# Twelve products with unread results ahead of tile 0's attention, and the prologue in another order

## The reference, cut to what matters

```python
# x: (16, 128, 64, 2); S4D-like token mixing gives h: (16, 128, 1024)
num = exp(dt_Lambda_neg) - 1
den = exp(dt_Lambda_neg * L) - 1
Wc = Wc * num * _reciprocal(den * Lam, EPS)                    # Wc from x
K = einsum('chn,hnl->chl', Wc, exp(dt_Lambda[..., None] * pos - P_max[..., None]))
h = K.real
# masked linear layer on the layer norm, 1024 x 1024, mask in blocks of 32 x 32
w_masked = weight * elem_mask
h = h + einsum('bsk,nk->bsn', _layernorm(h), w_masked)
# base layer 1024 x 1024 + router (8 experts, sparsemax) + LoRA of rank 16
z = _layernorm(h)
h = h + einsum('bsd,od->bso', z, W_base) + b_base + einsum('bser,bse,ero->bso', hA, weights, lora_B)
```

## Time and profile before

| what | us |
| --- | --- |
| median of 3 runs | 519.96 (519.64 to 520.29) |
| the profiled execution, device time | 520.99 |
| its span, first to last instruction | 519.2 |
| PE busy in the span | 480.4 |
| DVE busy | 408.4 |
| ACT busy | 261.4 |
| POOL busy | 125.7 |

### The profile page before, as it was taken

The page is one execution under the profiler, slowest core; times in us unless marked ns, Lnnn a source line. Parts: engine busy times, 40 slices in busy tenths (PEclk is TensorE's granted clock), DMA queues, the critical chain, the costliest instruction groups (busy, mean ns, idle before and its releaser), DMA issues.

```text
span 519.2 us, 7441 instructions
## 1 busy us (share of the span) xinstructions
PE 480.4 (93%) x2467; PEld 406.1 (78%) x2467; DVE 408.4 (79%) x862; ACT 261.4 (50%) x476; POOL 125.7 (24%) x110
## 2 busy tenths in 40 slices
PE   1378789999999999999999999999999999999995
PEld 0267667877888888888888888888888888888884
DVE  7998979898988888888888888888888888854241
ACT  2848887576464626364554646362636455232200
POOL 0765597440303021020303030302102030303020
PEclk9998989999999999999999999999999999999999
DMA  8993113040403031212212030403121211313011
GB/s 286 391 338 51 63 42 122 1 127 6 126 3 110 16 88 38 81 45 68 59 40 86 10 116 0 109 17 88 38 81 47 67 56 26 96 31 92 1 40 40
DMA packets 28764, 40.83 MB, mean 79 GB/s; under 512 B 10760, under 2 KB 21192, under 8 KB 28744
## 3 DMA queue, kind: packets, MB, share of 16 engines
q1 hardware_dynamic: 28368, 40.49, 25.8%
q10 hardware_dynamic: 376, 0.10, 0.1%
HBM read 23.80 MB, written 16.78 MB: 78 GB/s over the span
## 4 chain that ended last, share of the span: by engine, by line
PE 90%; DVE 4%; issue 2%; ACT 2%; DMA 1%; POOL 1%; SPq 0%; DVEq 0%; POOLq 0%; ACTq 0%
PE acc_b L455 38%; PE acc_a L455 34%; PE turnp L439 6%; PE small L479 4%; PE turnp L448 3%; PE small L481 2%; PE acc_b L420 1%; PE acc_b L399 1%; DMA mask_raw<-in_L_attn_mask 1%; PE xps L429 1%; ACT wa_hi L668 1%; DVE mask_sum L1071 0%; DVE wa_raw L1080 0%; DVE wa_lo L1087 0%; PE small L487 0%
## 5 line engine op out<-in xcount | busy, mean ns | idle before, releaser
L982 POOL TENSOR_TENSOR h<-h,st 128x1024 f32<-128x1024 f32 x16 | 30.4, 1897 | 325.1 <-PE turnp L448 321.5
L455 PE MATMUL acc_a<-wa_hi,x_hi 128*128 128x512 f32 x256 | 83.2, 401 | 1.9 <-DVE wa_lo L1087 1.9
L455 PE MATMUL acc_b<-wb_hi,x_hi 128*128 128x512 f32 x256 | 83.9, 404 | 0.0
L455 PE MATMUL acc_a<-wa_hi,x_lo 128*128 128x512 f32 x256 | 81.3, 394 | 0.0
L455 PE MATMUL acc_a<-wa_lo,x_hi 128*128 128x512 f32 x256 | 81.2, 393 | 0.0
L455 PE MATMUL acc_b<-wb_lo,x_hi 128*128 128x512 f32 x256 | 80.5, 390 | 0.0
L455 PE MATMUL acc_b<-wb_hi,x_lo 128*128 128x512 f32 x256 | 80.5, 390 | 0.0
L455 PEld LDWEIGHTS acc_a<-wa_hi,x_lo 128*128 128x128 f32 x256 | 48.6, 190 | 10.4
L752 ACT ACTIVATE x_hi<-turnp 128x1024 fp32r<-128x1024 f32 x16 | 16.4, 1024 | 79.4 <-PE turnp L448 79.4
L455 PEld LDWEIGHTS acc_a<-wa_lo,x_hi 128*128 128x128 f32 x256 | 48.5, 189 | 10.0
L455 PEld LDWEIGHTS acc_b<-wb_hi,x_lo 128*128 128x128 f32 x256 | 48.1, 188 | 10.4
(11 more groups left out here) (200 smaller groups left out, 937.0 us busy)
## 6 DMA issues: line engine op xcount, KB each, us to landing
h<-rows_out SPq DMA_DIRECT2D x16, 512.0 KB, 3.3
out<-h SPq DMA_DIRECT2D x15, 512.0 KB
rows_out<-b_sb SPq DMA_DIRECT2D x56, 128.0 KB, 2.3
mask_raw<-in_L_attn_mask SPq DMA_DIRECT2D x8, 512.0 KB, 9.9
wa_raw<-in_L_attn_weight SPq DMA_DIRECT2D x8, 512.0 KB, 10.5
wb_raw<-in_L_ffn_W_base SPq DMA_DIRECT2D x8, 512.0 KB, 6.7
rows_out<-tmp SPq DMA_DIRECT2D x8, 128.0 KB, 2.3
xn<-in_x SPq DMA_DIRECT2D x15, 64.0 KB
```

Of the source, the lines that this page charges most:

```text
L455: return pe.matmul(cols, a, rows, start=first, stop=last)
L982: pool.tensor_tensor(h2[par][:, :], h2[par][:, :], st2[:, par, 1:2].to_broadcast([P, L]), ALU.subtract)\
```

## The change

A new helper on PE issues fp32 products of the identity with 256 columns of the constants, whose results nobody reads (the first product of tile 0's attention overwrites them):

```diff
+            def keep_clock(bank, n):
+
+                for _ in range(n):
+                    pe.matmul(bank, ident, kst[:, 0:2 * P], start=True, stop=True)
```

Its calls, and the new place of the calls around them on PE:

```diff
             k_transposed(0)
+            block_sums(5)
+            block_sums(6)
             wa_half(6)
             wa_half(7)
-            block_sums(6)
-            block_sums(7)
+            pe.wait_ge(wa_masked, 3)
+            keep_clock(acc_a[:, HALF // 2:HALF], 2)
+            keep_clock(acc_a[:, HALF // 2:HALF], 2)
+            keep_clock(acc_a[:, HALF // 2:HALF], 2)
             wa_half(8)
+            keep_clock(acc_a[:, HALF // 2:HALF], 2)
+            keep_clock(acc_a[:, HALF // 2:HALF], 2)
             wa_half(9)
+            keep_clock(acc_a[:, HALF // 2:HALF], 2)
             pe.wait_ge(kt_lo, 1)
             wa_rows_ready(NWT // 2)
             first_attention(0, [0])
             first_attention(0, [1])
+            block_sums(7)
+            first_attention(0, [2])
             wa_half(10)
-            first_attention(0, [2])
+            x_transposes(1)
             first_attention(0, [3])
```

```diff
             parameters(0)
+            table_b(0)
             phases_1()
-            table_b(0)
```

On DVE nearly every call moves. At the start:

```diff
             dt_exponential()
             signs()
+            dec_and_turn()
+            q_arguments(0)
+            reciprocal_of_tanh(0)
+            phases(0)
             mask_sums(0)
-            dec_and_turn()
-            phases(0)
-            q_arguments(0)
+            mask_sums(1)
             wa_mask(0)
-            reciprocal_of_tanh(0)
```

More of the change, by code:

```diff
@@ L528, in _ @@
             block_sums(0)
+            pe.wait_ge(rt_in, 16)
+            pe.transpose(small[:, HALF - rt_rows:HALF], rt_stage, ident[0:rt_rows, 0:rt_rows]).then_inc(rt_t, 1)
             block_sums(1)
@@ L531, in _ @@
             wa_half(0)
+            wa_half(1)
             block_sums(3)
-            wa_half(1)
+            x_transposes(0)
             block_sums(4)
[L535 to L538, removed]
             wa_half(2)
@@ L588, in _ @@
             attention(1, 0)
+            wb_half(6)
+            wb_half(7)
+            attention(1, 1)
             wb_half(8)
             wb_half(9)
-            attention(1, 1)
             attention(1, 2)
@@ L602, in _ @@
             attention(1, 6)
+            wb_half(13)
+            wb_half(14)
             attention(1, 7)
-            wb_half(14)
             wb_half(15)
+            k_transposed(2)
             pe.wait_ge(h2t_lo, 1)
@@ L612, in _ @@
             base(0, 0)
+            x_transposes(3)
             base(0, 1)
@@ L779, in _ @@
             q_tanh(0)
+            x_rows_twice(0)
+            q_sines(0)
+            sines(0)
+            exponentials(0)
+            wa_centre(0)
+            wa_highs(0)
             act.wait_ge(ldt_in, 16)
@@ L797, in _ @@
             wa_highs(4)
+            x_rows_twice(1)
+            exponentials(1)
             wa_highs(5)
+            wa_centre(4)
             k_high(0)
@@ L802, in _ @@
             wa_raws(3)
+            wa_centre(5)
             wa_highs(8)
-            x_rows_twice(1)
             wa_highs(9)
-            exponentials(1)
-            wa_centre(5)
+            q_tanh(1)
             sines(1)
@@ L813, in _ @@
             wa_highs(13)
-            q_tanh(1)
             wa_highs(14)
             wa_highs(15)
[L817 to L822, removed]
             k_sum(0)
             k_deviation(0)
+            wb_highs(0)
             q_sines(1)
+            x_rows_twice(2)
+            k_high(1)
+            wb_highs(1)
             wb_highs(2)
             wb_highs(3)
-            k_high(1)
+            sines(2)
             wb_highs(4)
@@ L851, in _ @@
             act.activation(lb_hi[:, :], lb_raw[:, :], ACT.Copy).then_inc(lorb_hi, 1)
-            k_high(2)
+            sines(3)
+            gated_high(0)
             exponentials(3)
-            gated_high(0)
-            sines(3)
             h2_deviation(1, 1)
@@ L1298, in _ @@
             signs()
+            dec_and_turn()
+            q_arguments(0)
+            reciprocal_of_tanh(0)
+            phases(0)
             mask_sums(0)
-            dec_and_turn()
-            phases(0)
-            q_arguments(0)
+            mask_sums(1)
             wa_mask(0)
-            reciprocal_of_tanh(0)
-            mask_sums(1)
             mask_sums(2)
             mask_sums(3)
+            decay_b(0)
+            reciprocal_of_norm(0)
             wa_mask(1)
-            reciprocal_of_norm(0)
-            mask_sums(4)
+            wa_lows(0)
+            v_factors(0)
             wa_mask(2)
             wa_mask(3)
-            wa_mask(4)
-            decay_b(0)
-            v_factors(0)
+            mask_sums(4)
+            wa_lows(1)
             mask_sums(5)
-            wa_lows(0)
-            wa_lows(1)
             table_v(0)
             mask_sums(6)
+            wa_mask(4)
             wa_lows(4)
             wa_lows(5)
+            phases(1)
+            q_arguments(1)
+            k_low(0)
             mask_sums(7)
             wa_mask(5)
-            phases(1)
-            k_low(0)
             wa_mask(6)
+            k_turn(0)
             wa_lows(8)
+            wa_mask(7)
             wa_lows(9)
-            q_arguments(1)
-            wa_mask(7)
             decay_b(1)
-            k_turn(0)
+            reciprocal_of_tanh(1)
             wa_lows(12)
@@ L1341, in _ @@
             wb_lows(0)
+            phases(2)
+            k_low(1)
             wb_lows(1)
-            phases(2)
-            reciprocal_of_tanh(1)
+            wb_lows(2)
             h1_reciprocal(0)
-            wb_lows(2)
             wb_lows(3)
@@ L1349, in _ @@
             attention_residual(0, 0)
-            k_low(1)
             wb_lows(4)
             wb_lows(5)
+            k_turn(1)
             wb_lows(6)
+            router_columns()
             wb_lows(7)
-            k_turn(1)
+            decay_b(2)
+            reciprocal_of_norm(1)
             wb_lows(8)
             wb_lows(9)
-            reciprocal_of_norm(1)
+            v_factors(2)
             wb_lows(10)
+            table_v(2)
             wb_lows(11)
             wb_lows(12)
+            h2_low(0)
             wb_lows(13)
[L1363 to L1366, removed]
+            h2_reciprocal(0, 0)
             wb_lows(14)
             wb_lows(15)
+            h1_reciprocal(1)
             phases(3)
-            h2_reciprocal(0, 0)
-            h1_reciprocal(1)
             dve.wait_ge(b_ready, 3)
```

53 lines of the change are left out of this document (21 added, 32 removed).

## The result

The changed kernel takes 521.86 us (median of 7 runs, 520.23 to 523.54); the kernel before, beside it, 519.96 (7 runs, 519.63 to 520.55). The ratio is 1.0035, with a 95% interval of 1.0018 to 1.0052: a loss of 0.35%, small, but the interval leaves out 1. The forecast was 516.5. The profiled execution took 521.86 us with a span of 520.1 (before: 520.99 and 519.2).

A forecast was written before the change was run, and what follows sets the result against it. TensorE is busy from 118.02 us on, so only idle and half-clock time before it can move: -1.5 + (7.5 - 7.6) + (1.7 - 3.4) = -3.3, and 0.2 for POOL: -3.5 from 519.96 gives 516.5 us, range 514.3 to 520.3.

The forecast's parts named there:

- Part 1: The start, on DVE: v_sb ends at 29.6, k_transposed(0) starts at about 29.7 and ends at 33.1, 3.3 us earlier.
- rival D: At the start, everything waits for xn on ACT's queue: slower, 522.5 us if it lands at 17.1; chance 0.08.
- Part 2: Twelve multiplications ahead of tile 0's attention cost 1.7 of the 3.2 us gained; attention starts at 40.6, -1.5 us.
- rival B: Clock still low in the twelve multiplications, so attention starts near 43.7: 518.5 us; chance 0.17.
- Part 3: Tile 0's attention to k_transposed(1): wb_half(0) at 51.7 after 2.0 us idle; k_transposed(1) waits 2.5 us for b_sb(1), at 56.7.
- Part 4: From k_transposed(1) to 118 us: waits of 2.35, 0.88 and 1.20 us go, new ones of 1.6 us come.
- the step in part 4: At wb_half(13): table_v(2) waits for tile 1's rows, DVE loses 1.1 us, yet wb_lows(11) is done at 80.2.
- the booked fall: One half-clock spell on PE behind the idle times 49.7 to 51.7 and 54.2 to 56.7, costing 1.7 us.
- the small waits: New PE waits after k_transposed(1): 0.3 us for the residual, then 0.4, 0.4, 0.3, 0.2 at wb_half(8) to (11); 1.6 us.
- Rival C: At k_transposed(3), DVE or the rows' round trip is late, 3.5 us idle, prologue's gain lost: 519.9 us; chance 0.10.
- The last paragraph of the prediction: What the profile after would show, and what could be wrong: a DVE queue running later than counted beside other POOL work.

The follow-up runs named there:

- the lower group of times: Changed kernel with POOL's additions in table_b(2) and add_bias waiting for DVE: two executions at 514.89 and 514.96 us, the other four at 516.73 to 516.86.

## Why the prediction was wrong

**Right**, by its parts. Part 1: v_sb(0) ends at 29.22 (forecast 29.6), k_transposed(0) starts at 29.41 (29.7); xn held nobody up, so rival D is out. Part 2: a product of 256 columns takes about 0.46 us at the upper clock (0.445), the rows of all twelve add up to 5.7 us (5.3), and rival B did not occur. Without them attention starts at 38.94, where 38.9 was forecast; with them at 39.62 and not 40.6, so they cost 0.7 us and not 1.7. Part 3: wb_half(0) at 51.33 (51.7), k_transposed(1) at 56.39 behind 2.37 us (56.7, 2.5). Part 4 up to DVE's wait for tile 1's rows: attention(1, 0) waits 0.35 us for the residual (0.3), the rows are there at 76.01 (75.9). No wait ahead of wb_half(6), and no fall at 43 or 70.

**Wrong: the step in part 4** by which wb_half(13) "still finds wb_lows(11) done at 80.2", and the one after it, by which the queue reaches table_b(3) 5 us earlier. Both price table_v at three operations of 1.22 us. The third took 3.28 and 3.44, wb_lows(11) began at 81.61, and k_transposed(3) started at 117.27, not 114.5.

The price was read from tile 0's row, and that is another operation: `v_sb<-turnp,v_sb`. For tiles 0 and 1 table_v puts its second product into turnp, one of PE's banks, from tile 2 on into tmp in SBUF. In the kernel before, tile 0's addition ran its 1.22 us at 30.00 in the middle of POOL's addition of 29.30; tile 2's, which reads tmp, took 1.66 and ended 1.08 us behind the POOL operation of 84.85. POOL before the change:

```profile
29.30 2.35 POOL L933 TENSOR_TENSOR b_sb<-b_sb,h 128x1024 f32<-128x1024 f32 x1
...
84.85 1.94 POOL L931 TENSOR_TENSOR h<-pp,qq 128x1024 f32<-128x1024 f32 x1
```

and DVE:

```profile
86.21 1.66 DVE L1167 TENSOR_TENSOR v_sb<-tmp,v_sb 128x1024 f32<-128x1024 f32 x1
```

From the forecast to the measured span, behind k_transposed(1), which came 0.3 us early: 1.9 and 2.1 us idle at 82 and 117, 1.6 for the fall at 83, less 1.7 for the booked fall that did not come, less 0.8 because the small waits were 0.35, 0.22 and 0.26 instead of 1.6, puts k_transposed(3) 2.8 us later (117.27 instead of 114.5). The fall over it adds 1.6: 4.4 us. -3.5 + 4.4 = 0.9, which is 521.86 - 520.99. With both additions of POOL held back the sum is met: 516.75 us in the median, where 516.5 was forecast, and k_transposed(3) at 113.9 without a wait. Such a close fit is in part luck: the 516.5 came from 517.5 for a profiled execution by the 1.03 us between profile and median of the kernel before, while here the profiled one took 516.86, near its median. The order is worth about what part 4 said; what was missing is who else is at work at the moment to which an operation is moved. Rival C had the place of the last wait right, k_transposed(3) waiting for DVE, but not the reason.

The last paragraph of the prediction names it ("table_b and tensor_tensor stretch when they meet") and gives it neither a place nor a price nor a chance. The rows were there to price it: besides the 1.66 us at 86.21 the trace of before has a POOL addition of 3.47 us beside DVE at 110.24. Two meetings of up to 2.2 us on DVE's queue were due among the rivals, with a chance of slower well above 0.13. At the second meeting the decision is sharp: DVE 20 ns ahead in the kernel before, POOL 40 ns ahead in the changed one.

**The clock**: one fall was booked behind the two waits of 49.7 to 56.7, at 1.7 us. In the profile of after none came there; in other kernels with the same waits it came at 51 and was free, or at 57 and cost 1.8. The size was right; its place and whether it is paid were not to be had from a sum. The 1.7 us booked were not spent there, and two falls that were not booked came at 83 and 117.

## To carry to other kernels

Where an edit moves a vector operation that reads two SBUF tiles, lay DVE's and POOL's timelines beside each other at its new place, see in which memory its operands lie at that place (another tile's row may be of another operation), and price the later of two that meet at its own time plus all that is left of the other; where it matters, let a semaphore decide which is first rather than some tens of nanoseconds. Fill a wait of PE to hold the clock only if PE sets the time of what follows: here nine products in the waits of 49.5 to 56.6 brought 1.7 us in the median (against the lower group of times nothing), and twelve ahead of attention nothing. When several versions lie 2 us apart with spread in each, look at which of their executions have a fall that is paid, before reading a median as an effect of the edit.

## What was not expected of the hardware

- The one that is second stands still for the whole rest of the first, in both directions: DVE 1.22 to 2.89, 2.93, 2.97, 3.28, 3.43 and 3.44 us beside POOL's 2.40; POOL 2.40 to 3.47 beside DVE's 1.23; even a DVE operation of 0.29 us (128 x 128) becomes 2.51 beside POOL's lb_lo. A lead of 20 to 50 ns is enough in these records. And it is not only operations with two tiles: in the kernel before, a TENSOR_SCALAR of DVE on one tile (lb_raw from dec, 128 x 112) took 1.15 us at 42.15 beside POOL's 1.13 at 42.09, where the one behind it took 0.27.
- Executions of one program have their falls at different places. Up to 76 us the changed kernel and six of the others (the edits of those come later) are the same program, and of their seven profiles three have a fall at 51, three at 57, and the changed kernel's none up to 83. The place goes with that of the first rise: k_transposed(0), over which the clock rises, took 2.64 to 2.70 us in the first three, 3.60 to 3.64 in the second three and 3.17 in the changed kernel. That the times of one kernel differ by this fits (514.9 and 516.8 with the same mean clock of 0.993, so both with a fall), but of no kernel were executions of both groups profiled. The Trainium skill ("TensorE: Matmul & The Clock Gate", Part 1) says that the chip's look at PE's activity runs freely beside the kernel, so that the moment of a change varies from run to run. Of the rise at the start it tells this, and these seven profiles show it of the falls as well.
- Nine unread products in the idle stretches (4.2 us of PE time) moved the work behind them by under 0.2 us (wb_half(0) at 51.49, k_transposed(1) at 56.58), and the spread of the times shrank from 2 to 0.3 us with the twelve (four executions) and to 1.1 without them (four).

What stays open: why tile 1's rows came 2.1 us later in one execution than in another with the same fall, where the kernel before loses 0.2% by the twelve products, and in which share of the executions of the changed kernel each fall occurs, since only one execution of each was profiled.
